# Squares of the weighted values on ScalarE, the scaling read from PSUM one step later, two late gains on GpSimd

## What is computed

```python
x = x + _L0_xattn_ref(_layernorm(x), ctx, ctx, ...)      # 16-head cross-attention
x = x + _L0_attn_ref(_layernorm(x), ...)                 # attention by learned positions
x = x + _L0_ffn_ref(_layernorm(x), ...)                  # mixture of 8 experts, 2 picked, one shared
x = x + _L1_xattn_ref(_layernorm(x), ctx, ...)           # norm g1, attention, norm g2, feed-forward, norm g3
x = x + _L1_attn_ref(_layernorm(x), ...)                 # differential attention across the heads, feed-forward
x = x + _L1_ffn_ref(_layernorm(x), ...)                  # product keys, 50 candidates a head
```

```python
att2 = att6[:, :, 0, :, 0, :] - lam * att6[:, :, 1, :, 1, :]
out = jnp.einsum('bnah,bhnd->bnad', att2, v)
out = _rmsnorm(out) * (1.0 - LAMBDA_INIT)     # x * rsqrt(mean(x * x) + eps) over the 16 features of a head
return out.reshape(b, n, d) @ Wo.T + bo
```

## Time and profile before

| | us |
|---|---|
| median of 3 runs | 3420.44 |
| lowest and highest of them | 3415.87, 3421.91 |
| the profiled execution, its own time | 3419.78 |
| its span, from the first instruction to the last | 3417.7 |
| VectorE busy in it | 1929.2 (56%) |
| TensorE busy | 2563.9 (75%) |
| ScalarE busy | 922.6 (27%) |
| GpSimd busy | 667.3 (20%) |

### The profile page before, as it was taken

One profiled execution on the slowest core, in us unless ns is written; L12 is line 12 of the kernel. 1 busy time (PEld: TensorE's weight loads), 2 busy tenths in 40 slices (PEclk: granted clock), 3 DMA queues, 4 the chain that ended last, 5 costly groups with the idle time before them and its releaser, 6 DMA issues. The chain is left out here.

```text
span 3417.7 us, 47357 instructions
## 1 busy us (share of the span) xinstructions
PE 2563.9 (75%) x16384; PEld 1837.5 (54%) x16384; DVE 1929.2 (56%) x7470; ACT 922.6 (27%) x1994; POOL 667.3 (20%) x572
## 2 busy tenths in 40 slices
PE   5786888578984888858885789848888588866553
PEld 3584567345863557535674457635585356743331
DVE  2313455855747438564558556484385645683458
ACT  1212242123322233222421233212322224212210
POOL 0102114112221113021141122211130211411140
PEclk8698999789996899969997889969999799976666
DMA  6175144141623235141441416322251414412100
GB/s 233 44 249 191 38 159 156 64 165 59 202 105 112 87 94 200 68 155 38 150 165 64 163 55 193 120 102 98 85 209 67 150 44 144 171 64 101 25 0 7
DMA packets 215092, 392.59 MB, mean 115 GB/s; under 512 B 83728, under 2 KB 167952, under 8 KB 189616
## 3 DMA queue, kind: packets, MB, share of 16 engines
q1 hardware_dynamic: 208688, 372.49, 31.6%
q0 software_dynamic: 6144, 16.79, 1.5%
HBM read 350.55 MB, written 38.67 MB: 114 GB/s over the span
## 5 line engine op out<-in xcount | busy, mean ns | idle before, releaser
L799 PE MATMUL ps<-xbT,stream 128*128 128x128 f32 x2560 | 325.6, 283 | 12.8 <-DMA stream<-in_experts 8.4
L799 PEld LDWEIGHTS ps<-xbT,stream 128*128 128x128 f32 x2560 | 312.7, 198 | 25.1 <-DMA stream<-in_experts 13.2
L301 POOL TENSOR_TENSOR hTB<-pb,sbuf 128x2048 f32<-128x2048 f32 x32 | 152.0, 4763 | 431.4 <-DVE pb L1660 431.4
L1016 PE MATMUL ps<-ident,work 128*50 128x128 f32 x32 | 12.3, 385 | 240.5 <-DVE work L1799 240.5
L610 PE MATMUL ps<-cmat,aTB 128*128 128x512 f32 x256 | 144.3, 716 | 39.9 <-DVE sbuf L1744 36.2
L473 POOL TENSOR_TENSOR rstdB<-veB,mhalf 128x4 f32<-128x4 f32 x48 | 48.8, 1017 | 631.0 <-DVE veB L1281 631.0
L602 PE MATMUL ps<-ident,xnB 128*128 128x128 f32 x256 | 55.6, 338 | 154.1 <-DVE xnB L1288 122.8
L473 POOL TENSOR_TENSOR rstdA<-veA,mhalf 128x4 f32<-128x4 f32 x24 | 24.4, 1017 | 736.9 <-DVE veA L1281 736.9
L513 POOL DMA_INDIRECT hTA<-y_slots,slot x64 | 63.2, 988 | 518.6 <-DMA y_slots<-yb 501.5
L799 PE MATMUL ps<-xbT,ctxA 128*128 128x128 f32 x1280 | 158.2, 277 | 2.2 <-DMA ctxA<-in_experts 1.9
L799 PEld LDWEIGHTS ps<-xbT,ctxA 128*128 128x128 f32 x1280 | 150.8, 192 | 12.7 <-issue 5.2
(11 more groups left out here) (277 smaller groups left out, 5972.3 us busy)
## 6 DMA issues: line engine op xcount, KB each, us to landing
stream<-in_experts SPq DMA_DIRECT2D x88, 1024.0 KB, 5.1
stream<-in_experts SPq DMA_DIRECT2D x88, 512.0 KB, 5.9
ctxA<-in_experts SPq DMA_DIRECT2D x40, 1024.0 KB, 5.1
work<-in_ctxT SPq DMA_DIRECT2D x32, 1028.0 KB, 7.2
hTB<-in_ctxN SPq DMA_DIRECT2D x32, 1024.0 KB, 7.1
down<-in_experts SPq DMA_DIRECT2D x40, 512.0 KB, 5.9
ctxA<-in_ctxT SPq DMA_DIRECT2D x16, 1024.0 KB, 9.1
stream<-in_ctxT SPq DMA_DIRECT2D x16, 1024.0 KB, 10.7
```

The source lines that it names most:

```text
L301: return e.tensor_tensor(out.rearrange("p (a d h) -> p a d h", a=8, d=16), a.unsqueeze(2).broadcast_to([P, 8, 16, 16]), vals[:, t, :].rear ...
L799: ins = mm(ps[:, 2 * (b % 2) + u, f * P:(f + 1) * P], wu[:, u, k, f * P:(f + 1) * P], xbT[:, b % 2, k, :], start=k == 0, stop=k == KT - 1)
```

## The change

There are three edits. First, output() writes the sums into raw, which is PSUM bank 6 with room for two tiles, and ScalarE squares raw into the same place as before, at the second step of its turn; VectorE's mean_squares waits for it. Second, the scaling reads raw and writes ob, and it has moved from the second step of turn t+2 to the front of the first step, ahead of values(t+2). Third, the gains of y1 and y2 are multiplied by GpSimd, ahead of its bias additions.

```diff
+        raw = ps[:, 6, :].rearrange("p (s n) -> p s n", s=2)
...
                                 if slot == 1:
                                     for t in range(T):
-                                        pool.wait_ge(vec_done, V[tag, "g", t])
+                                        wait_scaled(pool, tag, t)
+                                        pool.wait_ge(pe_done, PE[tag, "T", t])
+                                        nc.gpsimd.tensor_tensor(dst[:, t], dst[:, t], w[gain], ALU.mult).then_inc(pool_done, O.step(tag, "g", t))
+                                    for t in range(T):
+                                        pool.wait_ge(pool_done, O[tag, "g", t])
                                         add(tag, t, dst[:, t], dst[:, t], w[be])
...
                         for i in range(T + 2):
                             yield
+                            if 1 <= i <= T:
+                                t = i - 1
+                                act.wait_ge(vec_done, V["pred", t, 1])
+                                if t >= 2:
+                                    act.wait_ge(vec_done, V["rms", t - 2])
+                                sa(squares[:, t % 2, :], raw[:, t % 2, :], ACT.Square).then_inc(act_done, A.step("squares", t))
                             yield
                             if i >= 2:
                                 o_turn("l4", i - 2, oTB, 7)
...
-                        yield from norm("y1", xnB, xnB, smallB, after=late_gain("y1", "g1"), early=True)
+                        yield from norm("y1", xnB, xnB, smallB, early=True)
...
                         def output(t, j, products):
-                            vv.tensor_reduce(ob[:, t, j * 128:(j + 1) * 128], products.rearrange("p (n h) -> p n h", h=16),
+                            vv.tensor_reduce(raw[:, t % 2, j * 128:(j + 1) * 128], products.rearrange("p (n h) -> p n h", h=16),
...
                         def mean_squares(t):
-                            v.wait_ge(pool_done, O["pprod", t])
-                            output(t, 1, prodP[:, t % 2, :])
-                            own_steps()
-                            vv.tensor_tensor(squares[:, t % 2, :], ob[:, t, :], ob[:, t, :], ALU.mult).then_inc(vec_done, V.step())
-                            own_steps()
+                            v.wait_ge(act_done, A["squares", t])
                             vv.tensor_reduce(mx[:, t % 2, 0:16], squares[:, t % 2, :].rearrange("p (a d) -> p a d", a=16), AX.X,
...
                         for i in range(T + 2):
-                            if i < T:
-                                values(i)
-                            yield
                             if i >= 2:
                                 t = i - 2
                                 v.wait_ge(pool_done, O["rms", t])
-                                o3 = ob[:, t, :].rearrange("p (a d) -> p a d", a=16)
-                                vv.tensor_tensor(o3, o3, b16(mx[:, t % 2, 0:16], 16), ALU.mult).then_inc(vec_done, V.step("l4", "o", t))
+                                v.wait_ge(vec_done, V["pred", t, 1])
+                                vv.tensor_tensor(ob[:, t, :].rearrange("p (a d) -> p a d", a=16),
+                                                 raw[:, t % 2, :].rearrange("p (a d) -> p a d", a=16),
+                                                 b16(mx[:, t % 2, 0:16], 16), ALU.mult).then_inc(vec_done, V.step("l4", "o", t))
+                            if i < T:
+                                values(i)
+                            yield
+                            if 1 <= i <= T:
+                                v.wait_ge(pool_done, O["pprod", i - 1])
+                                output(i - 1, 1, prodP[:, (i - 1) % 2, :])
                             if 1 <= i <= T:
                                 mean_squares(i - 1)
                             yield
```

More of the change, by code:

```diff
@@ L518, in back, with with_bias @@
                     def back():
-                        def with_bias(tag, be, dst):
+                        def with_bias(tag, gain, be, dst):
                             def then(slot):
@@ L534, in back @@
                             yield
-                        yield from norm("y1", veB, rstdB, with_bias("y1", "be1", xnB))
+                        yield from norm("y1", veB, rstdB, with_bias("y1", "g1", "be1", xnB))
                         for _ in range(T + 2):
                             yield
-                        yield from norm("y2", veB, rstdB, with_bias("y2", "be2", xnB))
+                        yield from norm("y2", veB, rstdB, with_bias("y2", "g2", "be2", xnB))
                         for t in range(T):
@@ L1303, in stats @@
                         vv.bn_stats(small[0][:, t, :], src[:, t, :]).then_inc(vec_done, V.step(tag, "st", t))
[L1305 to L1311, removed]
                     smallA, smallB = (stA, mvA, veA, rstdA, mrA), (stB, mvB, veB, rstdB, mrB)
@@ L1608, in ffn @@
                                 yield
-                        yield from norm("y2", xnB, xnB, smallB, after=late_gain("y2", "g2"), early=True)
+                        yield from norm("y2", xnB, xnB, smallB, early=True)
                         yield from ffn("y2", "y2b", xnB, None)
@@ L1701, in back @@
                         for i in range(T + 2):
+                            if i >= 2:
+                                t = i - 2
+                                v.wait_ge(pool_done, O["rms", t])
+                                v.wait_ge(vec_done, V["pred", t, 1])
+                                vv.tensor_tensor(ob[:, t, :].rearrange("p (a d) -> p a d", a=16),
+                                                 raw[:, t % 2, :].rearrange("p (a d) -> p a d", a=16),
+                                                 b16(mx[:, t % 2, 0:16], 16), ALU.mult).then_inc(vec_done, V.step("l4", "o", t))
                             if i < T:
@@ L1704, in back @@
                             yield
-                            if i >= 2:
-                                t = i - 2
-                                v.wait_ge(pool_done, O["rms", t])
-                                o3 = ob[:, t, :].rearrange("p (a d) -> p a d", a=16)
-                                vv.tensor_tensor(o3, o3, b16(mx[:, t % 2, 0:16], 16), ALU.mult).then_inc(vec_done, V.step("l4", "o", t))
+                            if 1 <= i <= T:
+                                v.wait_ge(pool_done, O["pprod", i - 1])
+                                output(i - 1, 1, prodP[:, (i - 1) % 2, :])
                             if 1 <= i <= T:
```

## The result

The changed kernel takes **3445.09 us** in the median of 4 runs (3442.11 to 3448.00). The kernel before took 3418.15 us beside it (4 runs, 3413.58 to 3421.91). The ratio is 1.0087, with a 95% interval of 1.0068 to 1.0106: slower by 23 to 36 us. The profiled execution took 3442.11 us.

What follows compares the result with a forecast made beforehand. VectorE was taken to bound the values stage, with TensorE halting for scaled tiles. 7 x 3.4 + 1.2 = 25.0 us on 3419.78, plus 0.66 to the median, gave 3445.4 us (48%); range 3426 to 3454.

Steps and rivals of the forecast that it cites:

- the wait for the power: Values stage: VectorE sits out GpSimd's power ahead of the scaling; chain 1.7 us later a loop turn, 1.2 last group.
- Squares: a loss of 0.1 us a chain: Values stage: squares on ScalarE instead of VectorE make each of the 32 chains about 0.1 us longer.
- The scaling at 0.43 us: Values stage: with one operand from PSUM each scaling takes 0.43 us, giving back 28.9 us over 32 calls.
- The copy behind the squares: ScalarE's oTB copy waits behind the next tile's squares, delaying TensorE's Wo: 3 us first, 3.8 us for tile 1.
- TensorE's clock: After the second halt, Wo and gate products take 1.76 and 3.01 us, 0.4 less than 2.07 and 3.09.
- A loop turn: 3.4 us: Values stage, TensorE: each of seven loop turns ends 3.4 us later, 3.8 from the copy's delay less 0.4.
- The late gains at nothing: Norms y1 and y2: moving 64 multiplications (34.5 us) from VectorE to GpSimd neither gains nor costs time.
- full clock: Rival, 25%: TensorE's clock stays full after the second halt; 1.7 us a turn, 13.1 in all, 3433.5 us.
- Faster: Rival, 7%: VectorE doesn't wait for the power, so the removed lock and gains in y2 count; 3382 us.
- the lock: Values stage: GpSimd's products block VectorE's two-SBUF-input scaling, 2.02 us instead of 0.43; removing it frees 28.9 us.
- No change: Rival, 10%: lock and wait cancel and the second halt ends sooner, some 3 us less a turn; 3421 us.
- longer low clock: Rival, 10%: another set of expert products and Wo of tile 2 run slow; 5.5 us a turn, 3460 us.

Runs made afterwards that it cites:

- e7: e5 with sums, squares and scaling in SBUF (ob) in place of PSUM, same order: 3461.86 us, ratio 1.0151 to the kernel before.
- e3: Changed kernel with ScalarE's copy oTB of tile t ahead of the squares of tile t+1: 3438.99 us, ratio 1.0060 to the kernel before.
- e4: Changed kernel with VectorE's scaling of tile i-2 moved between the products of tile i and their sum: 3405.60 us, ratio 0.9973 to the kernel before.
- e1: Kernel before with only the gains of y1 and y2 moved to GpSimd: 3414.38 us, ratio 0.9985.
- e2: Changed kernel with the late gains put back on VectorE: 3440.18 us, ratio 1.0058 to the kernel before.
- e5: Changed kernel with the edits of e4 and e3 together: 3397.65 us, ratio 0.9948 to the kernel before.

## Why the prediction was right, and where it was not

The forecast was 3445.4 us, and 3445.09 came. That the two are 0.3 us apart is luck. The sum had 25.0 us in the stages, where 20.7 came; 6.6 us that it hadn't came in the stretches between, -4.7 by scatter ahead of the first stage; and the kernel before took 3418.15 us beside the changed one and not the 3420.44 from which the sum starts. The direction and the wait for the power are right. The part that the sum gave to the copy is not what made the time.

- **Squares: a loss of 0.1 us a chain.** Wrong in sign, and small. From the start of the sum to the mean it is 3.19 us (520.94 to 524.13), against 3.23 before. The activation takes 0.38 us, not the 0.48 of the one over 257 columns with a bias from SBUF that I took it from the earlier trace rows.
- **The scaling at 0.43 us.** Right: 0.40 to 0.42 in the 32 calls, 13.4 us in all. e7 shows why. The rule of the Trainium skill named in the prediction (SBUF — State Buffer, Who interferes with whom) agrees with both ends: 4.71 us with two SBUF inputs, 0.42 with one.
- **The wait for the power.** Right for tile 0: 2.45 us ahead of it where I had said 2.3. For tile 1 I had said 2.3 too, and it is 0.36, as VectorE stands 1.77 us for Wo of tile 0 before. The chain is as forecast all the same. From scaling to scaling it is 11.95 and 11.37 us (527.35, 539.30, 550.67), forecast 12.07 and 11.47. The power of tile 3 starts 45.25 us into the stage (554.45 - 509.20); I had 45.8, or 1.7 us later than before, and it is 1.2. In the last group the stage grew by 0.63 us and not 1.2, for the same reason: each link is 0.1 to 0.2 us shorter than I had it.
- **The copy behind the squares.** There, and as large as forecast for tile 0: the wait for oTB is 5.15 us (forecast about 5). For tile 1 it is 1.94 (2.5 or more). Wo of tile 1 begins 38.39 us into the stage, 3.25 later than before; forecast was 3.8. But it is not what the turn is longer by: in e3 both waits are gone and the turn is as long.
- **TensorE's clock.** The size is right, the picture is not. I had both steps behind the second halt partly slow, 1.76 + 3.01 = 4.77 us. What came is Wo at full rate and the gate products low, 1.13 + 3.52 = 4.65. The first halt costs clock as well, 2.08 + 3.62 for what took 1.13 + 1.95; the prediction was silent on this, and the halt before tile 1 absorbs it. The Trainium skill (TensorE: Matmul & The Clock Gate, section on HAM oscillation) tells of a kernel in which each long wait for data makes the next burst of products start cold, that is at half rate. The halt of 5.15 us agrees: Wo behind it took 2.08 us. The waits of that section are longer than 1.94 us; behind the halt of 1.94 us Wo ran at the full rate, and the low level came with the products behind it.
- **A loop turn: 3.4 us.** In the stage it is 2.8 (52.71 - 49.88), so 20.1 us over seven turns (20.7 - 0.6) and not 23.8. Over the whole turn it is 3.4 (402.77 - 399.36), as forecast, but the path was another: I had made the copy the later of two and given it the 3.4, with 1.7 for the power. Without the copy's delay (e3) the turn still takes 402.76 us, and with it, but without the power wait (e4), 397.63. The power wait is sufficient for the 3.4, since TensorE then halts for the scalings and runs at the lower clock behind.
- **The late gains at nothing.** Right, by e1: its interval leaves room for a gain of 11 us and for no loss of more than 1.
- **What I did not have.** The stretches between the stages grew by 6.6 us. I had nothing for them. 3.3 of it lie in the last one (284.0 to 287.3 us) and belong to the edits of the values stage, as e1 (284.2) and e2 (287.1) show; where in that stretch they arise is open. For the rest, single stretches of the kernel before differ by 5.7 us among themselves (346.78 to 352.45), and e2, with the same stage, has 3.6 us less in them than after. I assign none of that rest to an edit.

Of the rivals, "full clock" had the chain of VectorE alone set the stage; the low rows behind both halts speak against it. "Faster" needed a power that VectorE doesn't wait for; it waits 2.45 us. Its count of the lock was right as busy time: the 32 scalings take 29.3 us less (42.7 - 13.4), for 28.9. Its time of 3382 us was not reached even with the wait out of the way: e4 is 9 us faster than before and e5 17. "No change" and "longer low clock" did not occur. The ends of the range are each about 1 us off: the middle of no change and full clock is 3427 and not 3426, that of the forecast and longer low clock 3453 and not 3454. This changes nothing here.

## What to carry to other kernels

A wait that is moved ahead of an engine's long work can cost nearly its full length in a step. If a result is needed by a short instruction, put the longest independent instruction between request and use; here one exchange in VectorE's order turned 27 us slower into 9 us faster (e4, 3 to 15). Where an instruction on VectorE with two SBUF inputs meets long GpSimd work, taking one input from PSUM is worth more than it looks (0.42 against 4.71 us), but that gain is only seen when the order that it forces has been paid for. Look also at what stands behind the new instruction on its own engine: a square of 0.38 us held TensorE for 5.15 us, because it waited for a later tile than the copy behind it. And measure a whole turn, not only the stage that was changed: putting the copy first took 1.0 to 1.3 us off the stage and nothing off the turn.

## What was not expected of the hardware

- A halt of TensorE can be paid for behind its first burst. After 1.94 us of idle time Wo ran at full rate (1.13 us, granted clock 1.00 over 547.59 to 548.55 us), and the 16 gate products behind it took 3.52 us (0.52 over 548.55 to 552.07, that is the lower level of 1.2 GHz for nearly all of them).
- A halt of one length had three outcomes. The 2.69 us ahead of tile 3 were followed by Wo at the lower level (2.08 us, e3), by Wo at full rate with the gate products low (3.42 us, e5, turn 2), and by both at full rate (e5, turn 1).
- The same instructions ran at either level in different turns of one kernel. In e5 the first 16 products L913 of a turn took 1.09 us in the stretch behind stage 1 and 1.95 in the one behind stage 2, TensorE by time:

```profile
755.59 1.09 PE L913 MATMUL ps<-hTB,pT 128*32 128x256 f32 x16
...
1153.01 1.95 PE L913 MATMUL ps<-hTB,pT 128*32 128x256 f32 x16
```

  In e5 the stretches between the stages differ with it, 349.9 against 353.2 us, in all of the first six; in e4 one of the six doesn't follow (1.09 us in a stretch of 351.9). Whether these products cause the difference or only go with it is not shown. So the total can take back what a stage gives: e3 lost 7.6 of 7.4 us, e5 half of 30.
- ScalarE's square of 256 columns takes 0.38 us from PSUM and 0.42 from SBUF (e7).
